# Two waits between a group's scatters: the eight row scatters of the dispatch in two bursts of four

## What is computed

```python
x = x + tanh(g_xattn) * xattn(layernorm(x), ctx)      # ctx: 192 columns, 128 keys per batch
#   q = h @ Wq; k, v = ctx @ Wk, Wv; softmax(q k^T / 8) v @ Wo + bo
x = x + tanh(g_ffn) * moe(layernorm(x))
#   scores = softmax(xf @ gate_w.T); the two best experts of each row
#   loc  = the row's rank among those that chose the expert (first choices before second)
#   disp[expert * cap + loc] = row  if loc < cap
#   eo = relu(disp @ fc1^T + b1) @ fc2 + b2
#   out = sum over the two experts of eo[row's place] * gate
```

## Time and profile before

| | |
|---|---|
| median of three runs | 1035.96 us (1035.08 to 1039.14) |
| the profiled execution | 1036.79 us, span from first to last instruction 1034.9 us |
| mean granted TensorE clock | 0.968 of full speed |
| TensorE busy (matmuls) | 962.2 us, 93% |
| VectorE, ScalarE, GpSimd busy | 642.1 us (62%), 504.6 (49%), 359.9 (35%) |
| the eight groups of the first stage | to about 600 us |
| the 64 dispatch scatters (L395) | 65.0 us, mean 1015 ns |

### The profile page before, as it was taken

One profiled execution on the slowest core, in us unless ns is written; L12 is line 12 of the kernel. 1 busy time (PEld: TensorE's weight loads), 2 busy tenths in 40 slices (PEclk: granted clock), 3 DMA queues, 4 the chain that ended last, 5 costly groups with the idle time before them and its releaser, 6 DMA issues.

```text
span 1034.9 us, 18912 instructions
## 1 busy us (share of the span) xinstructions
PE 962.2 (93%) x7158; PEld 838.1 (81%) x7158; DVE 642.1 (62%) x1517; ACT 504.6 (49%) x1564; POOL 359.9 (35%) x319
## 2 busy tenths in 40 slices
PE   7799998998998998999989977699999999999996
PEld 5587887887877877878868865599999999999995
DVE  5677586685785785875865764455555555554553
ACT  3576465564563663663763631345353535434352
POOL 6711025024033042051031053064554626355553
PEclk8999999999999999999998998899999999999999
DMA  8195002011020020020110011542426244242522
GB/s 249 44 284 165 22 30 75 22 58 45 22 78 28 21 88 16 22 78 6 42 42 23 20 40 44 163 122 47 127 42 161 76 101 123 47 119 42 134 61 31
DMA packets 63097, 76.60 MB, mean 74 GB/s; under 512 B 6033, under 2 KB 55096, under 8 KB 63008
## 3 DMA queue, kind: packets, MB, share of 16 engines
q1 hardware_dynamic: 50720, 59.18, 18.8%
q0 software_dynamic: 12288, 16.23, 7.9%
HBM read 46.52 MB, written 29.49 MB: 73 GB/s over the span
## 4 chain that ended last, share of the span: by engine, by line
PE 70%; ACT 10%; DVE 8%; POOL 4%; issue 3%; DMA 2%; another core or an unknown queue 2%; SPq 1%; POOLq 0%; DVEq 0%
PE down L1164 6%; PE down L1163 6%; PE down L1165 6%; PE up L1149 6%; PE up L1150 6%; PE up L1151 6%; PE out_bank L521 4%; PE probT L508 4%; PE score L533 4%; ACT probs_odd L690 3%; ACT work L690 3%; PE rT L1133 2%; PE query_bank L454 2%; PE query_bank L452 2%
## 5 line engine op out<-in xcount | busy, mean ns | idle before, releaser
L1095 POOL DMA_INDIRECT out_dram<-eo,index x64 | 105.1, 1642 | 98.3 <-ACT eo L1207 70.2
L1199 ACT ACTIVATE hid<-up,b 128x512 f32<-128x512 f32 x128 | 88.3, 690 | 84.4 <-PE up L1151 79.7
L690 ACT ACTIVATE work<-score,negmax 128x128 f32<-128x128 f32 x256 | 91.0, 380 | 48.8 <-DVE negmax L869 43.5
L690 ACT ACTIVATE probs_odd<-score,negmax 128x128 f32<-128x128 f32 x256 | 91.1, 382 | 47.7 <-DVE negmax L869 47.7
L395 POOL DMA_INDIRECT disp<-packed,slots x64 | 65.0, 1015 | 126.9 <-DVE slots L860 109.8
L1259 DVE TENSOR_TENSOR eo_raw<-down,b 128x256 f32<-128x256 f32 x64 | 26.0, 424 | 123.3 <-PE down L1165 123.3
L877 DVE COPY pT<-probT 128x512 f32<-128x512 f32 x128 | 82.3, 682 | 31.8 <-remote 21.8
L661 ACT ACTIVATE k_sb<-key_bank 128x512 f32<-128x512 f32 x64 | 39.0, 609 | 127.7 <-PE key_bank L477 127.7
L869 DVE TENSOR_REDUCE negmax<-score 128x4 f32<-128x512 f32 x128 | 82.2, 680 | 23.8 <-PE score L533 13.7
L533 PE MATMUL score<-k_sb,q_sb 64*128 64x128 f32 x1024 | 72.3, 282 | 26.1 <-ACT q_sb L661 25.6
L533 PEld LDWEIGHTS score<-k_sb,q_sb 64*128 64x128 f32 x1024 | 68.0, 193 | 33.2 <-ACT q_sb L661 30.6
(11 more groups left out here) (231 smaller groups left out, 2835.5 us busy)
## 6 DMA issues: line engine op xcount, KB each, us to landing
rows<-disp SPq DMA_DIRECT2D x18, 516.0 KB, 5.7
w_raw<-fc1T_dram SPq DMA_DIRECT2D x9, 1024.0 KB, 7.0
w_raw<-fc_dram SPq DMA_DIRECT2D x9, 1024.0 KB, 11.5
disp<-fixed SPq DMA_DIRECT2D x1, 8256.0 KB, 34.1
rows<-x_dram SPq DMA_DIRECT2D x16, 512.0 KB, 4.2
out_dram<-rows SPq DMA_DIRECT2D x8, 512.0 KB, 2.9
c_raw<-ctxT_dram SPq DMA_DIRECT2D x8, 256.0 KB
c_raw<-ctxT_dram SPq DMA_DIRECT2D x16, 128.0 KB
```

The lines of the kernel that those rows point to most:

```text
L690: last = nc.scalar.activation(probs[w % 2][:, c, :], score[hh][:, b * P:(b + 1) * P], ACT.Exp, bias=negmax[:, w % 2, c:c + 1], accum_out=s ...
L1095: pool.indirect_dma_start(out=out_rows[:, :], out_offset=bass.IndirectOffsetOnAxis(ap=index[half][:, i:i + 1], axis=0), in_=eo[half][:, i, ...
L1199: nc.scalar.activation(hid[m % 2][:, :], up[m % 2][:, :], ACT.Relu, bias=b1[par][:, m:m + 1]).then_inc(s_hid, 1)
```

## The change

In groups 1 to 6 GpSimd now waits twice more inside `dispatch`: ahead of the first four scatters for the scores of the group's last step, ahead of the second four for the scores of the next group's first step. In groups 7 and 8 (the last runs behind all steps) nothing changes.

```diff
--- before.py
+++ after.py
@@ -391,6 +391,8 @@
             pool.wait_ge(s_packed, g)
             pass_gate(pool, s_pool_gate)
             for j in range(2):
+                if g < NG - 1:
+                    pool.wait_ge(s_s_ready, 2 * NP * (g + 1) + 2 * j)
                 for b in range(GB):
                     pool.indirect_dma_start(
                         out=disp[:, :], out_offset=bass.IndirectOffsetOnAxis(ap=slots[:, j, b:b + 1], axis=0),
```

## The result

The changed kernel takes 1008.12 us (median of four runs, 1005.55 to 1011.17) against 1035.52 of the kernel before beside it: a ratio of 0.9726, with a 95% interval from 0.9702 to 0.9750. The forecast was 1015 with a range from 1009 to 1038.

A forecast was written before the change was run, and what follows sets the result against it. TensorE, busy 93% of the span, bounds the kernel, and scatter bursts hold up its results. Saving 4.2 us in each of five groups, 21 us, takes the profiled 1036.8 to 1015.8, less 0.8: 1015 us; range 1009 to 1038.

The forecast's parts named there:

- The place and the remedy: Eight scatters per group delay TensorE's results in the next group's second step; a gap after four saves 4.2 us per group.
- Rival (1): The gap before the fifth scatter does not open, since the count arrives at +4.9; hold-up stays, 1036 us; chance 0.22.
- Rival (2): The hold-up lasts while scatters are in flight, until 1.5 us after the last; 10 us more, 1046 us; chance 0.15.
- Rival (3): Half the effect: the step falls only to 8.6 us, the clock still falls; 1026 us; counted within the forecast's 0.63.
- The fifth scatter: Held by the second wait until about +6.9 us after the first scatter, instead of +5.25; the count arrives at about +6.
- step j1: Second step of the group following a burst: falls from 10.46 us to about 7.5, the length of the step before it.
- the saving of group 1: First burst, in group 1: its count was prompt, so nothing is saved there; 4.2 us in each of the other five.
- the slack of a step: How late VectorE's maxima may come without lengthening a step: about 1.8 us free, from the step with the late load.
- The clock term: TensorE's clock falls from 1.00 to 0.61 behind the burst, costing 1.6 us per group; 0.3 left for the second tail.
- What stood behind the wait: GpSimd's later `add_bias` and `rstd`: VectorE may wait up to 4.8 us more, covered by the projection on TensorE.
- six groups at 4.5: Lower end of the range: all six groups save up to 4.5 us each, giving 1009 us.
- On contention: By the skill's rule that DMA never contends with compute engines, the gap would move nothing, 1036 us; the trace speaks against it.

The follow-up runs named there:

- e1: Changed kernel with only the first wait, ahead of the first four scatters, kept: 1036.14 us, ratio 0.9994 to the kernel before.
- e2: Changed kernel with only the second wait, ahead of the second four scatters, kept: 1008.67 us, ratio 0.9739 to the kernel before.
- e3: Changed kernel with, in place of its waits, one ahead of the second four scatters for a count already waited for: 1037.40 us, ratio 1.0003.
- e5: Kernel before plus a GpSimd addition in a spare tile between fourth and fifth scatter of groups 1 to 6, no wait: 1003.86 us, ratio 0.9670.
- e6_spaced: Kernel before plus a small GpSimd operation ahead of every scatter of groups 1 to 6, no wait: 1022.46 us, ratio 0.9846.
- e7_narrow: Kernel before with each scatter writing 64 of 258 columns into its own table: one run, `aT_h` released 11.59 us after the first scatter.

## Why the prediction was right, and where it was wrong

**The place and the remedy** were right: a remote wait of the takers, on the burst's own clock, a step too long behind it, and a fallen clock behind that. `e1`, `e2`, `e3` and `e5` each changed one thing and moved the time only with the pause. Rival (1), that the pause does not open, is refuted by the pause of 1.4 to 1.9 us in five groups; `e3_passed_wait` shows what rival (1) looks like: 1037.4. Rival (2), that the hold lasts as long as scatters are under way, is refuted by the changed kernel's own timeline: the fifth scatter starts at 234.73, and `aT_h` is taken at 236.05 with no idle time. Rival (3), half the effect with a fallen clock, happened in `e6_spaced` (j1 8.8 to 8.9, clock down); group 6 of the profile after had its step (8.54) but not its clock.

**The fifth scatter** was forecast at +6.9 and came at +6.43 to +6.87 in groups 1 to 5: the arrival of the count at about +6 was well sized.

What failed are two terms of the sum: the length to which step j1 falls (7.5 us, measured 6.7) and the saving of group 1 (nothing, measured 4.84 us). Both made the gain too small.

**Mis-sized: the floor of step j1.** The forecast let it fall to 7.5 us, the length of j0, "with the same TensorE work". Measured 6.67 to 6.72 in groups 1 to 5. The same work does not make the same length: in the step before, TensorE stands idle 0.43 us for `q_sb` and 0.26 us for VectorE's `xT_l`, which takes the results of the group's two transposes; in j1 of the profile after it has no idle time.

```profile
227.96 1.09 PE L521 MATMUL out_bank<-pT,v_sb 128*64 128x128 f32 x16 [0.26 <-DVE xT_l L761]
```

The right neighbour was the step after the projection, 6.6 us in each group. In groups 2 to 5 this is 0.8 us each, 3.1 us in all; with j2 and the rounding they saved 20.8 us where 16.8 were forecast. The same floor made the slack of a step too large: by it the step with the late load (8.58 us, maxima 2.90 late) was 1.1 over, which left 1.8 us free; over 6.7 it was 1.9, which leaves about 1.0 (my estimate from the same rows). The 0.87 us by which the maxima came late still fit into it.

**Wrong: group 1.** "Nothing in the first, whose count was prompt." The prompt maxima of the earlier trace rows showed the count at 160.60, after the end of the fourth scatter at 160.58; I forgot there the 0.86 us from a release to the next scatter, which I had used for the other groups. That alone makes a pause of 0.9 us. It was 1.41, and the group saved 4.84 us. The forecast also overlooked that this burst was held up like the others in the kernel before: its step j1 was the longest of the six (10.52), and only its maxima were prompt.

**The clock term** was right in kind and nearly in size: 1.6 less 0.3 was forecast for each of groups 2 to 6, 6.5 in all; their steps j2 gave back 1.27 to 1.80, 7.6 in all. In group 2 the scores, L521 and L508 behind them take 1.57 us less. **Group 6** fell short in all, 3.66 for 4.2, by its short pause. With 4.0 more in groups 2 to 5, 4.8 in group 1, 0.5 less in group 6, and the traces' other differences of 3.8 against it, 21 becomes the 25.4 of the spans. The medians, with 27.4, stand 2.0 higher than the one profiled execution, which was the slowest of its four.

**What stood behind the wait** was covered, as said. `add_bias` starts 14.25 us after the first scatter instead of 12.75, and VectorE then waits for `rstd` in j2, 2.06 us of the up to 4.8 feared, beside the projection:

```profile
247.67 1.39 DVE L782 TENSOR_SCALAR rows<-rows,mv,rstd 128x256 f32<-128x256 f32 x4 [2.06 <-POOL rstd L329]
```

**The range** took its lower end from six groups at 4.5 us, which rests on the same floor of 7.5. With 6.7 it would have been 5.3 a group, 32 us, 1004: the bound of an unknown was taken from one neighbour only.

**On contention**: the Trainium skill, "SBUF — State Buffer", section "Who interferes with whom", says that DMA never contends with a compute engine. The change moved the time (0.9726), so the time that the prediction read out of that rule, 1036, did not come: in the first pair and the first two sets something on the scatters' side did delay what TensorE's results release, up to 11.6 us after the first scatter. That does not refute the rule for the ports of the SBUF, which is what that section is about: a quarter of the bytes left the hold as it was (`e7_narrow`, 11.59 us). In the last three sets no trace shows a delay.

**What stays open** is what the hold-up is, and why it was there on three occasions and not on three others. One more trait goes with it. The traces of the first pair and the first two sets hold between 6271 and 6668 records of semaphore updates, those of the last three sets 7430 to 7443, for nearly the same program. That the missing ones are the reason for the "remote" releasers is likely, but not shown. It would fit a path for such events that is overloaded on some occasions; but `e5_work_gap` has as few records (6501) and no hold in groups 1 to 6, so the loss is no measure of the hold, and this too is argued, not shown. All timed runs here were recorded for clock and span. So a rival is left that no run tests: that the recording is part of the hold-up, and that an unrecorded execution of the kernel before does not have it.

## What to carry to other kernels

Several engines that wait at once for results which the producer's own row says are finished, and that are all released at a fixed distance behind a run of scatters, point to the run, whatever names the profile gives as releaser. Try one pause of a microsecond or a little more after the fourth: here a piece of GpSimd work did it at least as well as a wait, and where there was nothing to gain the changed kernel's pause cost nothing measurable. Measure on more than one occasion, since the same change brought 2.7% on one and nothing on another. And when a stalled step is to shrink, take its new length from the shortest steps with the same work, not from the one beside it.

## What the runs showed of the hardware

- Eight indirect DMAs at 1.28 us from start to start held TensorE's results up to 11.6 us after the first (1.5 us after the last one's end); a pause of 1.15 us after the fourth took it away (`e5_work_gap`). One of 0.83 us, seen in one group of one execution, left half of it in j1. An even spacing of 1.43 us brought the release to 8.9 us and j1 from 10.4 to 8.9, but left j2 as it was.
- The hold does not depend on the bytes: 256 in place of 1032 for each row left it at 11.59 us (`e7_narrow`).
- TensorE's granted clock fell from 1.00 behind each of the six held bursts (0.61 in the window from 245 to 247, where TensorE had been busy 0.87 of the 2 us from 241), and behind none of them with the pause.
- The same program took 1035.5 to 1037.2 us on three occasions and 1000.6, 1003.8 and 1003.1 on three others, a difference of 3.2 to 3.7%, larger than the gain of the change (2.7%). The five sets were on five chips; whether the chip decides is not shown.
- A wait for a count already reached cost GpSimd's scatters nothing: the fifth started 5.26 us after the first with it and 5.25 without.
